# A fused two-layer attention kernel: a new order of work with chunks of 1, 2, 2, 2 and 1 groups, two-operand VectorE forms and split transfers

## The chip, the cores and the metric

The kernel runs on one core of one Trainium2 chip. The metric is the device time of one execution in microseconds (us); a measurement is the median of several executions. Engines are called PE (matrix), DVE (vector), ACT (scalar), POOL (GpSimd) and SP (sync, which issues DMAs); ACT issues DMAs too.

## The reference

The input is `x` of 32 sequences with 32 positions and 128 features. Two layers follow one another.

```python
# layer 0: conditioned transformer block, 16 heads of 8 features
cmod = silu(c) @ w_ada + b_ada                 # shift, scale, gate for both halves
qkv  = modulate(ln(x), shift_msa, scale_msa) @ w_qkv
w    = softmax(q / 8 . k);  y = w @ v
x    = x + gate_msa * (y @ w_proj + b_proj)
h    = gelu(modulate(ln(x), shift_mlp, scale_mlp) @ w_mlp1 + b_mlp1)
x    = x + gate_mlp * (h @ w_mlp2 + b_mlp2)
# layer 1: graph attention, 16 heads, 2 directions, keys are the first 20 positions
self_feat = concat(x, q_exp) @ W_self.T + b_self      # q_exp is 0 where a row of x sums to 0
for d in range(2):
    A    = (adj, or adj with its axes swapped)[:, :, :20, :]
    aff  = where(A.sum(-1) > 0, (q_d . k_d) / sqrt(8), NEG) + (A @ w_bias + b_bias)
    out += einsum(softmax(aff) @ self_feat[:, :20], Wout_d) + bout_d
x = x + relu(self_feat + out)
```

## The kernel before, in words

All arithmetic is float32. The 32 sequences are 8 *groups* of 4 sequences, so a group is 128 tokens. In layer 0 the normalization and the q, k, v products work on *chunks* of groups (`CHUNKS`), here of 1, 1, 2, 2 and 2 groups; from the projection on, everything works on four *mids* of two groups (`MIDS`). One *unit* is the attention of one group (units 0 to 7, layer 0) or of one group and direction (units 8 to 23, layer 1: group 0 has units 8 and 9, and so on). Units are handled in *sets* (`SETS`) that share one softmax pass: sets 0 to 4 belong to layer 0, and sets 5 to 12 to layer 1, one for each group with both directions. Mid m of layer 1 holds the units 8+4m to 11+4m.

A set runs through: `scores` (PE, 32 small products for a group and direction, each two PE instructions since the data is float32) into `ps_s`; in layer 1 `badd` (DVE, adds the bias and frees `ps_s`); `max` (DVE); `sub` (DVE or POOL); per unit `turn` (PE transposes), `exp` (ACT) and `values` (PE); then `recip` and `mult` (DVE). `ya` adds the two directions, `oT` transposes back, `fin1` and `fin2` (DVE) finish, and `store` writes.

The order is written out: `ORDER` is one list of (stage, key), `ON` says which engine does a step, and each engine takes its own steps from the list in that order, waiting on semaphores for what it needs and for buffers to come free. Nothing overtakes on an engine. `BANKS` gives each product one of four PSUM banks.

The names that the change touches:

- `stats` (DVE) takes mean and variance of a chunk, `rstd` (POOL) the power -0.5, `apply` normalizes (here POOL, one instruction per group), `dense xnT` transposes on PE, `take xnT` (DVE) multiplies by the scale and `shift` adds the shift; then come the products q, k and v and their `take`s. `vmask` writes a masked copy of v. A `take` of `k` is four masked copies, here all on ACT.
- `spread (v1, m)` copies the layer-1 values of mid m into the block layout `Vz1` by eight small DMAs, all issued by SP. `Vz1` has two slots (`V1_RING`), so the spread of mid 2 waits until the `values` of mid 0 (units 8 to 11) are done, and that of mid 3 until those of mid 1 (units 12 to 15) are. The `values` of a mid wait for its spread.
- `WARM` transposes of the identity run on PE at the start.
- `nmr` is minus mean times rstd, which ACT needs for a normalization by scale and bias.

## Time and profile before

| | |
|---|---|
| runs shown | 99.52, 98.32, 98.66 us; median 98.66 us |
| profiled execution | 97.58 us, span 95.8 us |
| granted TensorE clock, mean | 0.995 |
| busy in the span | PE 80.1 us, DVE 71.3, POOL 56.1, ACT 39.6 |

The span runs from the first to the last instruction of the profiled execution; 1.8 us of its own time lie around it. Busy times say how loaded an engine is, not what ends the kernel: that is read from waits and from the chain of work that ended last. A matmul's busy time includes its latency, so a PE that is busy without a break may still not be at its peak.

### The profile page before, as it was taken

To read this page: it belongs to the slowest core of one execution; us is meant where nothing else is said; L and a number is where in the kernel's file an instruction comes from. 1 tells how busy PE (TensorE), PEld (TensorE's weight loads), DVE (VectorE), ACT (ScalarE), POOL (GpSimd) and SP (SyncE) were. 2 spreads that over 40 slices of the span, in tenths; PEclk is the share of its full clock that TensorE was granted. 3 is DMA by queue.
4 is the path that set the end of the run, shared out by engine and by line. 5 is a ranking of instruction groups with operands and counts; after the bars stand their busy time and mean duration, and the time that the engine had idled before them with its cause. 6 is when DMAs were issued, how large, how long until landed. Compare 5 with 4: busy or idle time off the path is not lost.

```text
span 95.8 us, 4031 instructions
## 1 busy us (share of the span) xinstructions
PE 80.1 (84%) x1762; PEld 63.7 (66%) x1762; DVE 71.3 (74%) x176; ACT 39.6 (41%) x87; POOL 56.1 (59%) x70
## 2 busy tenths in 40 slices
PE   3519799899769999999999999999998698649620
PEld 3319487576558647787898887998787586537510
DVE  3980858987887999858856578986998779487491
ACT  0910076947506007955244406607383073225200
POOL 6799949999970983953530551964049176733030
PEclk9999999999999999999999999999999999999997
DMA  1999991000000000000000210002100011121303
GB/s 32 253 355 270 388 405 62 7 0 0 10 7 0 7 0 0 7 0 0 3 7 0 43 24 17 3 0 38 31 14 7 7 43 31 31 43 21 114 10 110
DMA packets 4034, 5.75 MB, mean 60 GB/s; under 512 B 720, under 2 KB 3152, under 8 KB 3888
## 3 DMA queue, kind: packets, MB, share of 16 engines
q1 hardware_dynamic: 3584, 4.96, 17.0%
q10 hardware_dynamic: 432, 0.52, 1.5%
q8 instruction: 14, 0.23, 1.1%
q14 instruction: 4, 0.03, 0.1%
HBM read 4.22 MB, written 0.52 MB: 50 GB/s over the span
## 4 chain that ended last, share of the span: by engine, by line
PE 56%; SPq 13%; POOL 10%; DMA 7%; DVE 6%; issue 5%; POOLq 0%
SPq L797 12%; PE ps_b L956 8%; PE ps_b L962 7%; PE ps_s L1018 6%; DMA w_ada_sb<-in_w_ada 5%; POOL Vz L734 4%; PE ps_b L885 4%; PE ps_b L969 4%; PE ps_b L973 4%; PE ps_b L1062 3%; PE ps_b L902 3%; PE ps_b L936 3%; PE ps_b L975 2%; PE ps_b L1054 2%; PE ps_b L980 2%
## 5 line engine op out<-in xcount | busy, mean ns | idle before, releaser
L712 POOL TENSOR_TENSOR E<-E,neg_max 128x640 f32<-128x640 f32 x7 | 9.4, 1346 | 5.6 <-DVE neg_max L1334 5.6
L1148 ACT ACTIVATE PT<-ps_b 120x384 f32<-120x384 f32 x16 | 7.3, 488 | 11.8 <-PE ps_b L1029 11.5
L744 POOL TENSOR_TENSOR Kb<-k_raw,head_mask 128x640 f32<-128x640 f32 x5 | 6.3, 1254 | 8.9 <-DVE k_raw L1246 5.4
L1089 ACT ACTIVATE Kb<-ps_b,head_mask 128x256 f32<-128x256 f32 (+1 forms) x20 | 7.0, 438 | 7.6 <-PE ps_b L936 7.6
L1326 DVE TENSOR_TENSOR E<-ps_s,bias_head 128x640 f32<-128x640 f32 x8 | 6.6, 825 | 3.8 <-PE ps_s L1018 3.0
L1104 ACT ACTIVATE hidden<-ps_b,cols 128x256 f32<-128x256 f32 x16 | 7.3, 474 | 4.9 <-PE ps_b L956 4.7
L936 PE MATMUL ps_b<-xm,w_qkv_sb 128*128 128x256 f32 (+1 forms) x30 | 8.4, 421 | 0.5 <-DVE xm L696 0.5
L956 PE MATMUL ps_b<-xm,w_rest_sb 128*128 128x256 f32 x32 | 8.7, 387 | 0.0
L734 POOL TENSOR_TENSOR Vz<-v_raw,quad_mask 128x1152 f32<-128x1152 f32 (+1 forms) x5 | 8.5, 1729 | 0.0
L1054 PE MATMUL ps_b<-Vz,PT 120*32 120x54 f32 (+1 forms) x384 | 5.7, 207 | 3.3 <-issue 2.3
L1029 PE MATMUL ps_b<-ident,E 128*120 128x128 f32 x48 | 7.0, 279 | 1.2 <-DVE home_a L1370 1.2
L1054 PEld LDWEIGHTS ps_b<-Vz,PT 120*32 120x32 f32 (+1 forms) x384 | 4.8, 109 | 4.4 <-issue 4.1
L962 PE MATMUL ps_b<-hidden,w_rest_sb 128*128 128x256 f32 x32 | 7.7, 382 | 0.0
L1018 PE MATMUL ps_s<-Kb,home_b 32*32 32x80 f32 x512 | 7.4, 239 | 0.0
L936 PEld LDWEIGHTS ps_b<-xm,w_qkv_sb 128*128 128x128 f32 x30 | 5.8, 238 | 2.1 <-DVE xm L1201 0.8
L706 POOL TENSOR_TENSOR xT<-gated,xT 128x256 f32<-128x256 f32 x5 | 3.6, 730 | 6.1 <-DVE gated L1219 6.1
L846 POOL TENSOR_TENSOR rstd<-var_eps,minus_half 128x2 f32<-128x2 f32 (+1 forms) x9 | 6.1, 678 | 1.9 <-DVE var_eps L1180 1.7
L717 POOL TENSOR_TENSOR home_a<-home_a 128x128 f32<-128x128 f32 x6 | 2.7, 457 | 7.2 <-DVE home_a L1370 7.2
L696 POOL TENSOR_TENSOR xm<-xm,cmod 128x256 f32<-128x256 f32 (+1 forms) x7 | 4.1, 585 | 4.8 <-DVE xm L1201 4.8
L1018 PEld LDWEIGHTS ps_s<-Kb,home_b 32*32 32x32 f32 x512 | 5.5, 103 | 1.8 <-issue 1.3
L1334 DVE TENSOR_REDUCE neg_max<-E 128x32 f32<-128x640 f32 x8 | 6.5, 817 | 0.2
L852 POOL TENSOR_SCALAR xn_tok<-x_tok,meanvar,rstd 128x128 f32<-128x128 f32 x8 | 6.4, 801 | 0.5
(102 smaller groups left out, 191.1 us busy)
## 6 DMA issues: line engine op xcount, KB each, us to landing
w_rest_sb<-in_w_rest SPq DMA_DIRECT2D x1, 1088.0 KB, 10.1
home_a<-in_adj SPq DMA_DIRECT2D x2, 448.0 KB, 6.8
Vz<-v_raw SPq DMA_DIRECT2D x16, 33.8 KB
home_a<-in_adj SPq DMA_DIRECT2D x1, 512.0 KB, 8.1
xT<-in_xT SPq DMA_DIRECT2D x1, 512.0 KB, 10.6
out<-gated SPq DMA_DIRECT2D x3, 128.0 KB, 1.8
x_tok<-in_x_tok ACTq DMA_DIRECT2D x1, 256.0 KB, 4.5
w_ada_sb<-in_w_ada SPq DMA_DIRECT2D x1, 256.0 KB, 4.9
```

Of the source, the lines that this page charges most:

```text
L712: return engine.tensor_tensor(e, e, less_max(key), ALU.add)
L734: return engine.tensor_tensor(Vz0[:, :, bs, :, :].rearrange("p i b j w -> p i (b j w)"), v0_raw[:, bs, :, :].rearrange("p b j w -> p (b j ...
L797: sp.dma_start(Vz1[to, k, i, c:c1, 0:nb, :, :].rearrange("p c b d w -> p c (b d w)"), v1_raw[of, j:j + c1 - c, bs, :, :].rearrange("p c b ...
L936: return pe.matmul(ps[:, 0:n], w, xm[:, bs, :], start=True, stop=True)
L956: return pe.matmul(ps[:, 0:n], w_mlp1_sb[:, name[2], :], xm[:, bs, :], start=True, stop=True)
L962: ins = pe.matmul(ps[:, 0:n], w_mlp2_sb[:, j, :], hidden[:, h % HID_RING, j, 0:n], start=(j == js[0]), stop=(j == js[-1]))
L1018: ins = pe.matmul(ps_s[QUAD * b:QUAD * b + QUAD, j, u * nk:(u + 1) * nk], qT, Kb, start=True, stop=True)
L1029: ins = pe.transpose(ps[0:KR, c * P:(c + 1) * P], E1[:, r, u, c * KR:(c + 1) * KR], ident[:, :])
L1054: ins = pe.matmul(ps[QUAD * b:QUAD * b + QUAD, o + c * SIX * CW:o + c * SIX * CW + w], PT[0:rows, r, c, b * S:(b + 1) * S], V, start=True, ...
L1089: return act.activation(Kb0[:, part, bs, :], ps_bs, ACT.Copy, scale=head_mask[:, 1, part:part + 1])
L1104: return act.activation(hidden[:, h % HID_RING, j, 0:n], ps[:, 0:n], ACT.Gelu_apprx_tanh, bias=cols[:, R_MLP1 + j:R_MLP1 + j + 1])
L1148: ins = act.activation(PT[0:KR, r, 0:CH, :], ps[0:KR, 0:CH * P].rearrange("p (j t) -> p j t", t=P), ACT.Exp)
```

## The change

The code gains four things. `apply` can run on ACT (with `nmr` computed on DVE for layer 0 too). Three kinds of small DVE operation of one input (`plus1`, `masks`, `var_eps`) become `scalar_tensor_tensor` with two inputs that give the same values. A spread is cut in halves of four DMAs, each half a step of its own, and two of the eight halves are issued by ACT. `warm` steps can stand anywhere in PE's order, each two transposes of the identity.

```diff
+SPREAD_PARTS = [[(0, 0, 0, 0, CH), (1, 1, 0, 0, CH), (4, 0, CH, 0, 1), (4, 1, CH, 1, 1)],
+                [(2, 2, 0, 0, CH), (3, 3, 0, 0, CH), (5, 2, CH, 0, 1), (5, 3, CH, 1, 1)]]
-CHUNKS = [(0, 1), (1, 2), (2, 4), (4, 6), (6, 8)]
-SETS = [(0,), (1,), (2, 3), (4, 5), (6, 7), (8, 9), (10, 11), ...
-XLOADS = [(0, 1), (1, 4), (4, 8)]
-LOADS_SP = ['cols', 'ada0', 'qkv', 'ada1', 'adj0', 'adj1', 'adj2', 'rest', 'xT']
+CHUNKS = [(0, 1), (1, 3), (3, 5), (5, 7), (7, 8)]
+SETS = [(0,), (1, 2), (3, 4), (5, 6), (7,), (8, 9), (10, 11), ...
+XLOADS = [(0, 1), (1, 3), (3, 8)]
+LOADS_SP = ['cols', 'ada0', 'qkv', 'adj0', 'adj1', 'adj2', 'ada1', 'rest', 'xT']
-WARM = 6
+WARM = 11
- 'apply': 'pool',
+ 'apply': 'act',
- 'resid2': 'pool',
+ 'resid2': 'dve',
- 'shift': 'pool',
+ 'shift': 'dve',
+ 'sub': 'dve',
+ ('sub', 7): 'pool',
...
+ ('spread', ('v1', 2, 0)): 'act',
+ ('spread', ('v1', 3, 0)): 'act',
+        def spread_half(engine, name, m, half):
...
+            for i, quad, j, c, n in SPREAD_PARTS[half]:
+                engine.dma_start(Vz1[M * i:M * i + M, k, i, c:c + n, 0:nb, :, :].rearrange("p c b d w -> p c (b d w)"),
+                                 v1_raw[QUAD * quad:QUAD * quad + M, j:j + n, bs, :, :].rearrange("p c b d w -> p c (b d w)"))\
+                      .then_inc(spread_done["v1", m, half], 16)
+                elif stage == "warm":
+                    for i in range(2):
+                        ins = pe.transpose(ps_s[:, i, 0:P], ident[:, :], ident[:, :])
+                elif stage == "apply":
+                    for s in fresh("act", ("nmr", (0, key)), ("rstd", (0, key))):
+                        act.wait_ge(*s)
+                    for g in range(*CHUNKS[key]):
+                        ins = act.activation(xn_tok[:, g, :], x_tok[:, g, :], ACT.Identity, bias=nmr[:, 0, g:g + 1],
+                                             scale=rstd[:, 0, g:g + 1])
-                return dve.tensor_scalar(var_eps[:, layer, g0:g1], meanvar[:, layer, g0:g1, 1], LN_EPS, None, ALU.add)
+                v = meanvar[:, layer, g0:g1, 1]
+                return dve.scalar_tensor_tensor(out=var_eps[:, layer, g0:g1], in0=v, scalar=LN_EPS, in1=v, op0=ALU.add,
+                                                op1=ALU.max)
```

The whole `ORDER` and `BANKS` are new. Layer 1 now takes its sets in the order 6, 8, 5, 7, 10, 9, 11, 12 (before 5 to 12). On DVE there now also stand the `sub` of sets 5 and 6 (before that of set 7 alone), all four `resid2` (before one), most of the `shift`s of layer 0 (chunks 0, 1, 2 and 4; before 1 and 2) and one `vmask`, and two of the three layer-1 key masks (`k1mask`) that were on DVE are on POOL; three of the four layer-1 normalizations (`take x1tok`) move from DVE to ACT. Three places show how the rows of an engine moved.

PE at the start, before: identity transposes (`ident`), the modulation product (`w_ada_sb`), transposes of the normalized input (`xn_tok`), the q, k, v products (`w_qkv_sb`) and the first scores.

```order
L986 MATMUL ps_s<-ident 128x128 x6
L912 MATMUL ps_b<-silu_c,w_ada_sb 128x32 x6
L885 MATMUL ps_b<-ident,xn_tok 128x128 x4
L936 MATMUL ps_b<-xm,w_qkv_sb 128x256 x2
L885 MATMUL ps_b<-ident,xn_tok 128x128 x2
L936 MATMUL ps_b<-xm,w_qkv_sb 128x128 x3
L1018 MATMUL ps_s<-Kb,selfT 32x128 x32
```

The same place after the change.

```order
L992 MATMUL ps_s<-ident 128x128 x11
L918 MATMUL ps_b<-silu_c,w_ada_sb 128x32 x2
L998 MATMUL ps_s<-ident 128x128 x4
L891 MATMUL ps_b<-ident,xn_tok 128x128 x5
L942 MATMUL ps_b<-xm,w_qkv_sb 128x256
L891 MATMUL ps_b<-ident,xn_tok 128x128 x2
L998 MATMUL ps_s<-ident 128x128 x2
L942 MATMUL ps_b<-xm,w_qkv_sb 128x256 x3
L1027 MATMUL ps_s<-Kb,selfT 32x128 x32
```

The second part of the modulation product (4 of its 6) no longer stands ahead of the transposes, more identity transposes do, and the products ahead of the first scores are four of 256 columns instead of two of 256 and three of 128.

DVE in the first microseconds, before: statistics (`stats`, `meanvar`, `var_eps`), the modulation (`cmod`) and the first modulated input (`xm`).

```order
L1191 TENSOR_TENSOR cmod<-ps_b,cols 128x64
L1175 BN_STATS stats<-x_tok 128x6 x2
L1178 BN_AGGR meanvar<-stats 128x2 x2
L1180 TENSOR_SCALAR var_eps<-meanvar 128x2
L1201 TENSOR_TENSOR xm<-ps_b,cmod 128x256
L696 TENSOR_TENSOR xm<-xm,cmod 128x256
```

The same place after the change.

```order
L1197 BN_STATS stats<-x_tok 128x6 x2
L1200 BN_AGGR meanvar<-stats 128x2 x2
L1203 SCALAR_TENSOR_TENSOR var_eps<-meanvar 128x2
L1310 SCALAR_TENSOR_TENSOR nmr<-meanvar,rstd 128x2
L1310 SCALAR_TENSOR_TENSOR nmr<-meanvar,rstd 128x1
L1215 TENSOR_TENSOR cmod<-ps_b,cols 128x64
L1225 TENSOR_TENSOR xm<-ps_b,cmod 128x256
L704 TENSOR_TENSOR xm<-xm,cmod 128x256
```

The `nmr` that ACT's normalization waits for stands behind the statistics of four chunks; a third `nmr` row, alike, is left out here.

ACT in the last third, before: exponentials (`PT`), and copies of the layer-1 keys (`k_raw`) and queries (`home_b`).

```order
L1148 ACTIVATE PT<-ps_b 120x384 x2
L1115 ACTIVATE k_raw<-ps_b,bk_scaled 128x160
L1148 ACTIVATE PT<-ps_b 120x384
L1110 ACTIVATE home_b<-ps_b,cols 128x256
L1115 ACTIVATE k_raw<-ps_b,bk_scaled 128x160
L1110 ACTIVATE home_b<-ps_b,cols 128x256
L1148 ACTIVATE PT<-ps_b 120x384 x12
```

The same place after the change.

```order
L1170 ACTIVATE PT<-ps_b 120x384 x6
L1124 ACTIVATE k_raw<-ps_b,bk_scaled 128x160 x2
L1119 ACTIVATE home_b<-ps_b,cols 128x256
L776 DMA Vz<-v_raw 20x3x144 x2
L776 DMA Vz<-v_raw 20x144 x2
L1170 ACTIVATE PT<-ps_b 120x384 x3
L776 DMA Vz<-v_raw 20x3x144 x2
L776 DMA Vz<-v_raw 20x144 x2
L1170 ACTIVATE PT<-ps_b 120x384 x7
```

Four DMA issues (half a spread of mid 2) now stand ahead of the last ten exponentials, and four more (mid 3) ahead of the last seven.

## Rows read from the trace of the kernel before

**Rows 1.** Page, part 1: busy us, share of the span, instructions.

```profile
PE 80.1 (84%) x1762; PEld 63.7 (66%) x1762; DVE 71.3 (74%) x176; ACT 39.6 (41%) x87; POOL 56.1 (59%) x70
```

**Rows 2.** Busy time by stretches: PE, PEld, DVE, ACT, POOL, clock, DMA share, GB/s.

```profile
30.00:40.00 10.00, 9.89 (x208) 6.63 (x207) 8.95 (x28) 4.72 (x9) 6.84 (x7) 1.00 0.02 3
60.00:70.00 10.00, 10.00 (x200) 8.57 (x179) 8.44 (x15) 4.98 (x10) 4.94 (x4) 1.00 0.10 19
80.00:90.00 10.00, 6.74 (x255) 5.37 (x247) 6.43 (x14) 3.71 (x8) 3.88 (x6) 1.00 0.18 47
```

**Rows 3.** Chain that ended last, in order of time: start us, us, what.

```profile
64.64 0.43 PE ps_b L973 x2
65.07 0.27 PE ps_b L975 x2
65.34 0.33 PE ps_b L1029 x3
65.67 0.84 PE ps_s L1018 x49
...
71.10 0.54 PE ps_b L980 x4
...
74.98 0.32 PE ps_b L1054 x9
...
75.32 0.81 SPq L797
...
81.76 0.81 SPq L797
...
87.39 1.84 DMA Vz<-v_raw
```

**Rows 4.** Waits of SP's queue: what waited for whom, us, times, longest.

```profile
SPq L797 <- PE ps_b L1054: 4.8, 1, 4.8
```

**Rows 5.** Timeline of the last values: start us, us, engine, line.

```profile
89.36 1.25 PE L1054 MATMUL ps_b<-Vz,PT 120*32 120x54 f32 x96 [0.82 <-DMA Vz<-v_raw]
```

**Rows 6.** Timeline of the first 20 us: start us, us, engine, line.

```profile
0.80 1.38 ACTq L1070 DMA_DIRECT2D x_tok<-in_x_tok  x3
...
6.25 0.49 DVE L1175 BATCH_NORM_STATS2 stats<-x_tok 128x6 f32<-128x128 f32 x2 [0.21 <-DMA x_tok<-in_x_tok]
...
10.85 2.04 PE L936 MATMUL ps_b<-xm,w_qkv_sb 128*128 128x256 f32 x4 [0.55 <-DVE xm L696]
...
14.42 1.04 POOL L870 CAST home_b<-home_a 112x1024 f32<-112x1024 int32 x1
14.49 0.99 DVE L1180 TENSOR_SCALAR var_eps<-meanvar 128x2 f32<-128x2 f32 x1
...
19.11 1.13 PE L936 MATMUL ps_b<-xm,w_qkv_sb 128*128 128x256 f32 x4
```

**Rows 7.** Groups of instructions by line and shape: count, busy us, mean ns, idle before.

```profile
L1148 ACT ACTIVATE PT<-ps_b 120x384 f32<-120x384 f32 x16 | 7.3, 488 | 11.8 <-PE ps_b L1029 11.5
L1326 DVE TENSOR_TENSOR E<-ps_s,bias_head 128x640 f32<-128x640 f32 x8 | 6.6, 825 | 3.8 <-PE ps_s L1018 3.0 <-PE ps_b L1029 0.5
L1334 DVE TENSOR_REDUCE neg_max<-E 128x32 f32<-128x640 f32 x8 | 6.5, 817 | 0.2
L852 POOL TENSOR_SCALAR xn_tok<-x_tok,meanvar,rstd 128x128 f32<-128x128 f32 x8 | 6.4, 801 | 0.5
L734 POOL TENSOR_TENSOR Vz<-v_raw,quad_mask 128x1152 f32<-128x1152 f32 x3 | 6.3, 2114 | 0.0
...
L1359 DVE RECIPROCAL rden<-ps_b 128x32 f32<-128x32 f32 x11 | 3.9, 352 | 2.7 <-PE ps_b L1054 2.6
...
L1235 DVE STREAM_TRANSPOSE v_raw<-ps_b 128x512 f32<-128x512 f32 x4 | 2.8, 706 | 1.4 <-PE ps_b L980 1.4
```

**Rows 8.** Line 712 on POOL: shortest, median, longest ns, first and last start.

```profile
L712 POOL TENSOR_TENSOR E<-E,neg_max x7: 1272/1273/1785, 59.4 to 85.3; 128x640 f32<-128x640 f32 x7
```

**Rows 9.** Timeline at 59.4 us.

```profile
59.44 1.78 POOL L712 TENSOR_TENSOR E<-E,neg_max 128x640 f32<-128x640 f32 x1 [2.76 <-DVE neg_max L1334]
```

More of the change, by code:

```diff
@@ L68 @@
 K_POOL = set()
-WARM = 6
+WARM = 11
 ON = {'adjf': 'pool',
- 'apply': 'pool',
+ 'apply': 'act',
  'badd': 'dve',
  'bdir': 'dve',
- 'bhead': 'act',
+ 'bhead': 'pool',
+ 'bks': 'act',
  'bturn': 'dve',
@@ L86 @@
  'mult': 'dve',
+ 'nmr': 'dve',
  'pen': 'dve',
@@ L99 @@
  'store': 'sp',
- 'sub': 'pool',
+ 'sub': 'dve',
  'turn': 'pe',
@@ L103 @@
  'vmask': 'pool',
+ 'warm': 'pe',
  'ya': 'pool',
  'zero': 'pool',
+ ('adjf', 2): 'act',
+ ('bhead', 1): 'act',
  ('k1mask', (0, 1)): 'dve',
- ('k1mask', (1, 0)): 'dve',
- ('k1mask', (1, 1)): 'dve',
  ('resid1', 2): 'dve',
  ('resid1', 3): 'dve',
- ('resid2', 3): 'dve',
- ('shift', (0, 1)): 'dve',
- ('shift', (0, 2)): 'dve',
- ('sub', 0): 'dve',
- ('sub', 1): 'dve',
- ('sub', 2): 'dve',
- ('sub', 3): 'dve',
- ('sub', 4): 'dve',
- ('sub', 7): 'dve',
+ ('shift', (0, 3)): 'pool',
+ ('shift', (1, 1)): 'pool',
+ ('shift', (1, 2)): 'pool',
+ ('spread', ('v1', 2, 0)): 'act',
+ ('spread', ('v1', 3, 0)): 'act',
+ ('sub', 7): 'pool',
+ ('sub', 8): 'pool',
+ ('sub', 9): 'pool',
+ ('sub', 10): 'pool',
+ ('sub', 11): 'pool',
+ ('sub', 12): 'pool',
  ('take', (('cmod', 0), 0)): 'dve',
@@ L174 @@
  ('take', (('q', 0), 0)): 'act',
[L175 to L176 removed]
+ ('take', (('q', 1), 0)): 'dve',
+ ('take', (('q', 2), 0)): 'act',
  ('take', (('q', 3), 0)): 'act',
@@ L185 @@
  ('take', (('q1', 3, 0), 0)): 'act',
- ('take', (('q1', 3, 1), 0)): 'act',
+ ('take', (('q1', 3, 1), 0)): 'dve',
  ('take', (('rowsum', 0), 0)): 'dve',
@@ L783, in _ @@
                 if stage == "spread":
[L784 to L799 removed]
+                    spread_half(sp, "sp", *key[1:])
                 else:
@@ L1046, in _ @@
                         m = mid_of(g)
-                        for s in fresh("pe", ("spread", ("v1", m))):
+                        for s in fresh("pe", ("spread", ("v1", m, 0)), ("spread", ("v1", m, 1))):
                             pe.wait_ge(*s)
@@ L1092, in take_part @@
                 if kind == "x1tok":
-                    for s in fresh("act", ("nmr", h), ("rstd", (1, h))):
+                    for s in fresh("act", ("nmr", (1, h)), ("rstd", (1, h))):
                         act.wait_ge(*s)
@@ L1096, in take_part @@
                         ins = act.activation(xn_tok[:, g, :], ps[:, (g - g0) * P:(g - g0 + 1) * P], ACT.Identity,
-                                             bias=nmr[:, g:g + 1], scale=rstd[:, 1, g:g + 1])
+                                             bias=nmr[:, 1, g:g + 1], scale=rstd[:, 1, g:g + 1])
                     return ins
@@ L1112, in take_part @@
                 d = name[2]
-                for s in fresh("act", ("gbias", 0)):
+                for s in fresh("act", ("bks", 0)):
                     act.wait_ge(*s)
@@ L1127, in _ @@
                     continue
+                elif stage == "spread":
+                    spread_half(act, "act", *key[1:])
+                    continue
+                elif stage == "bks":
+                    for s in fresh("act", ("load", "cols")):
+                        act.wait_ge(*s)
+                    ins = act.activation(bk_scaled[:, :], cols[:, R_K:R_K + DIRS], ACT.Copy, scale=C ** -0.5)
+                elif stage == "apply":
+                    for s in fresh("act", ("nmr", (0, key)), ("rstd", (0, key))):
+                        act.wait_ge(*s)
+                    for g in range(*CHUNKS[key]):
+                        ins = act.activation(xn_tok[:, g, :], x_tok[:, g, :], ACT.Identity, bias=nmr[:, 0, g:g + 1],
+                                             scale=rstd[:, 0, g:g + 1])
                 elif stage == "adjf":
@@ L1243, in take_part @@
                 if kind == "k1":
-                    for s in fresh("dve", ("gbias", 0)):
+                    for s in fresh("dve", ("bks", 0)):
                         dve.wait_ge(*s)
@@ L1280, in _ @@
                 elif stage == "nmr":
-                    g0, g1 = MIDS[key]
-                    for s in fresh("dve", ("rstd", (1, key))):
+                    layer, p = key
+                    g0, g1 = norm_chunk(layer, p)
+                    for s in fresh("dve", ("rstd", key)):
                         dve.wait_ge(*s)
-                    ins = dve.scalar_tensor_tensor(out=nmr[:, g0:g1], in0=meanvar[:, 1, g0:g1, 0], scalar=-1.0,
-                                                   in1=rstd[:, 1, g0:g1], op0=ALU.mult, op1=ALU.mult)
+                    ins = dve.scalar_tensor_tensor(out=nmr[:, layer, g0:g1], in0=meanvar[:, layer, g0:g1, 0], scalar=-1.0,
+                                                   in1=rstd[:, layer, g0:g1], op0=ALU.mult, op1=ALU.mult)
                 elif stage == "apply":
```

415 lines of the change are left out of this document (204 added, 211 removed), and 10 rows, old and new, of the table ORDER.

## Prediction, before the changed kernel ran

> **What bounds the kernel now.** I read the busy time by stretches first. PE is busy without a gap from 30 to 70 us, and falls to 6.74 of 10 us at 80 [rows 2]; over the span it is the busiest engine [rows 1]. So there are three stages: a head in which PE waits, a middle that PE's work sets, and a tail. The chain of work that ended last confirms it. In the middle it is one PE piece behind another; at 75.30 us (I call it T0: the last `values` of units 8 to 11 end) it leaves PE, and SP issues sixteen DMAs one after another, eight from 75.32 and eight from 81.76; the last one lands 1.84 us after its issue, at 89.22 [rows 3]. SP had waited 4.8 us for those `values` [rows 4], since the two slots of `Vz1` were taken. The last four units' `values` run from 89.36 to 90.61 [rows 5], and 5.15 us later the span ends. From T0 to the end are 20.5 us, 13.9 of them issue and landing.
>
> **The tail.** The issues are as many as before, about 0.77 us each by the two runs of eight (81.76 - 75.32 = 6.44 with the wait between; 87.39 - 81.76 = 5.63). But half of each spread goes to ACT's queue. Walking the new order from T0:
> - PE takes two `q1` and a `k1` (0.43 + 0.27 + 0.43 [rows 3]), and ACT copies the last at about T0 + 1.65. ACT then issues four DMAs (3.1 us, to 4.75) while SP issues the other four. Behind ACT's stand the exponentials of units 13, 12 and 19 (0.49 each [rows 7], to 6.2), and with them the `values` 13 and 12 (to 6.05).
> - Now mid 1 is free. ACT issues four more (6.25 to 9.35), landed at 11.2 with the 1.84 of rows 3, and only then the exponentials of 18, 16, 17, 20 and 21 (to 11.8).
> - DVE is the second queue. From T0 to the `max` of set 12 it has 16 operations: three `badd` and four `max` (0.82 each, 5.7 together [rows 7]) and nine from 0.35 to 0.72 ([rows 7] give the two ends; 3.9 together), so the `max` ends at 9.85 with what is unfinished at T0. `sub` 12 on POOL takes 1.27 [rows 8], to 11.1; two `turn`s (0.33 each) end at 12.0 with the hand-over, and exponential 23 at 12.7.
> - The last `values` (0.31 a unit: 1.25 for four [rows 5]) end at 13.4, and 5.15 follow: 18.6, or 18.9 with 0.3 for hand-overs that I rounded off.
>
> So T0 to the end takes 18.9 instead of 20.5: **-1.6 us**. Both spreads have landed 1 us before they are wanted, and what comes last instead is DVE's queue, with ACT's 0.2 us behind it. Removing 6 us of serial issue gives back far less than 6, because the softmax chains of the last three sets are as long.
>
> **Work moved behind T0.** In the new order two `q1`, one `k1` and one `v1` stand behind T0 (0.86 + 0.27 + 0.54 = 1.67 us [rows 3]), and two units' `turn`s have gone ahead of it (0.66). In a stage that PE's work sets, T0 itself comes 1.0 us earlier: **-1.0 us**. The walk above has the moved work in it.
>
> **The head.** The first `k` product starts at 10.85 [rows 6]. In the new order it needs chunk 1 alone, but `nmr` of chunk 1 stands behind the statistics of four chunks, and two of these wait for the third load of `x`, which lands at about 6.25 or a little later (it grows from 4 to 5 groups) [rows 6]. Two statistics of 0.97 us each, from there, end at 8.3; ACT's normalization, transpose, scale and shift lead to a first product at about 10.5. That is 0.3 us earlier, not more, though POOL loses 6.4 us of `apply` (0.80 each [rows 7]). Next, `var_eps` took 0.99 us at 14.49, until the cast on POOL ended at 15.46 [rows 6]; the two-input form should take its usual 0.17, and POOL's `rstd` behind it comes 0.8 us earlier. The second modulation part no longer stands ahead of the transposes. Against that `adj` now loads ahead of it, and POOL has still 8.5 us of `vmask` and casts in the same 20 us.
>
> The PE clock decides the rest. Two-instruction products of 256 columns took 0.51 us each at 10.85 and 0.28 at 19.11 (2.04 and 1.13 for four [rows 6]), while the page lists the clock as full. By these times PE worked at its lower level, 1.2 GHz, in the first, and at 2.4 GHz in the second; it had been busy almost without a break from 10.85. If the new warm-up raises it by 10 us, my walk of the first attention has 1.5 us more PE work done at 36 us than before; if it rises where it did, none. I take **-0.5 us**, between 0 and -1.5, nearer to the unchanged case.
> The Trainium skill says in TensorE: Matmul & The Clock Gate, Part 4 (PE-mode transpose), that transposes do not count as PE activity for the clock. All the added warm-up is transposes. By that rule the head's gain is 0 and the time 0.5 us above my forecast; the row at 10.85, slow behind six such transposes, does not speak against it.
>
> **DVE in the middle.** DVE gets three `resid2`, more `shift`s, one more `sub`, `nmr` and a `vmask`, and loses three normalizations and two key masks: about +2 us on 71.3 [rows 1]. From the first layer-1 scores to T0 I count 12.9 us of DVE work for 14.0 us of PE work, 92%, where the stretch from 60 to 70 has 8.44 of 10 [rows 2]. PE will wait for it now and then: **+0.7 us**, between 0 and 1.5. The eleven identity transposes and two of the warm steps stand in time in which PE waits for `x`, and cost nothing; the third warm step stands among products and costs 0.2 us, which is in the head's term. The other edits (`bhead` to POOL, `bks`, `consts`) lie under PE's middle.
>
> **Sum.** -1.6 - 1.0 - 0.5 + 0.7 = -2.4 us. Against its own time that is 95.8 to 93.4 of span, 97.6 to 95.2 of the profiled execution; against the median of 98.66, which lies 1.1 above that execution, **96.3 us**, -2.4%. A measurement of this kernel tells about 2% (2 us) from no change.
>
> **Rivals.**
> - *POOL blocks DVE.* The moved `shift`, `sub`, `resid2` and `vmask` read two operands from SBUF on DVE, beside POOL's long ones. In the trace the one `sub` on POOL that ran beside such a DVE operation took 1.78 us instead of 1.27 [rows 8, 9], so 0.5 us for one meeting. A `shift` behind a fresh `vmask` (2.11 [rows 7]) would lose up to 2.1, ahead of `max` and `sub` of set 2, and three or four meetings on the path cost 1.5 to 2.5 us: 98.3 at the middle. The DVE queue would then be the bound from 20 us on. For it: DVE is already the tighter queue. Against it: most DVE work there reads PSUM.
>  SBUF — State Buffer, section Who interferes with whom, of the Trainium skill states this as a rule: a DVE instruction with two SBUF inputs and a GpSimd one that reads SBUF exclude each other for a whole instruction. It speaks for this rival, and by it the two-operand `var_eps` would still wait for a cast (0.8 us more than my sum), though not for a memset.
> - *ACT's issues hold the exponentials (slower).* In the tail ACT has 0.2 us of slack. If an issue there takes as long as SP's, the sum holds; ACT's own early ones took 0.46 [rows 6]. If both queues hinder one another and each issue doubles to 1.5 us, the two groups of four delay units 13 to 22 by 3.1 us each: 6.2 - 0.2 = +6.0, so 102.3 us, slower. The point from which it decides the sign is 0.77 + 2.4/8 = 1.1 us an issue.
> - *Faster still.* The clock rises early (-1.0 more), DVE's load hides (-0.7) and the `var_eps` wait was on the path of all later chunks (-0.8): 93.8 us.
> - *The change does not do what it says.* ACT's half of a spread stands behind copies and exponentials, so it may be issued later than SP's would have been. In my walk it is 1.65 us late for mid 2 and on time for mid 3; it would have to be 1 us later before a landing is last.
>
> **How the numbers follow.** Forecast case (95.0 to 97.4) 0.47; POOL blocks DVE (97.4 to 99.5) 0.24; faster still (below 95.0) 0.17; slow issues on ACT (above 99.5) 0.12. Faster than 96.7 (2%) is the third and three quarters of the first: 0.52. Slower than 100.6 is most of the last: 0.10. The rest, 0.38, is within 2%. Eight in ten: 93.9 to 99.8.
>
> **What the new profile would show.** The chain of the tail without SP; the last spread landed about 1 us ahead of the last `values`; T0 to the end about 19 us. T0 at 73.8 or a little before. First `k` product at 10.5; its instructions at 0.5 or 0.28 us tell the clock. `var_eps` never above 0.3 us. PE busy nearly all of 37 to 73, DVE near 9 of 10 in the last third. I am wrong if ACT's issues exceed 1 us, if PE shows gaps for DVE of more than 2 us together in the middle, or if the first attention ends later than before.

## The result, and the profile after

The changed kernel took 101.12 us (median of 4 runs, 100.09 to 101.57) beside 98.49 us for the kernel before on the same chip: ratio 1.031, interval 1.025 to 1.037. It is slower; I had forecast 96.3 us and given this side a tenth. The same kernel timed again in a later group of runs gave a ratio of 1.018 (1.006 to 1.029). Single executions of either kernel scatter by 1.5% and more; ratios are of undisturbed runs, medians of all runs, so the two do not always match. The profiled execution took 101.2 us, its span 99.4.

The windows that answer to [rows 2], and the same for the second profile of the same kernel and for before, from the end of T0's `values` to the end of the last ones (busy time of PE, PE's loads, DVE, ACT and POOL, then granted clock and DMA):

```profile
30.00:40.00 10.00, 8.96 (x220) 6.31 (x218) 7.87 (x26) 4.39 (x9) 5.15 (x7) 1.00 0.02 4
40.00:50.00 10.00, 9.26 (x46) 7.13 (x46) 7.78 (x27) 5.16 (x13) 2.29 (x5) 1.00 0.00 0
80.00:90.00 10.00, 7.16 (x261) 5.59 (x260) 6.01 (x12) 2.90 (x7) 5.49 (x7) 1.00 0.18 44
...
76.00:94.40 18.40, 15.55 (x530) 12.63 (x525) 11.74 (x25) 5.24 (x12) 9.04 (x11) 0.91 0.15 38
```

The second profile of the changed kernel:

```profile
76.20:92.45 16.25, 14.26 (x525) 11.46 (x526) 11.89 (x25) 5.12 (x12) 9.04 (x11) 1.00 0.14 36
```

The kernel before:

```profile
75.25:90.60 15.35, 11.97 (x523) 9.98 (x522) 10.84 (x25) 5.45 (x12) 6.80 (x8) 1.00 0.17 45
```

In the middle PE is no longer without gaps (8.96 and 9.26 where before had 9.89 and 9.96). And behind T0 it has 14.3 us of work up to the end of the last `values` (the second profile; the first, at a lower clock, has 15.6), 2.3 more than before. T0 is at 76.08 us (before 75.30; the sum of my terms puts it at 74.5) and T0 to the end takes 23.3 us (before 20.5; my walk 18.9). These two errors, 1.6 and 4.4, are the whole 6.0 us between my span of 93.4 and 99.4.

PE in the tail, timeline of the profile after (start, duration, instruction, and in brackets the idle time ahead and what ended it; "issue" means that PE waited for nothing that the profile shows):

```profile
75.66 0.40 PE L1063 MATMUL ps_b<-Vz,PT 120*32 120x54 f32 x17 [0.83 <-issue]
...
81.96 0.79 PE L1063 MATMUL ps_b<-Vz,PT 120*32 120x54 f32 x41 [0.26 <-ACT PT L1170]
83.49 0.27 PE L1063 MATMUL ps_b<-Vz,PT 80*32 80x36 f32 x7 [0.74 <-issue]
...
88.64 0.55 PE L1038 MATMUL ps_b<-ident,E 128*120 128x128 f32 x3 [1.75 <-ACT PT L1170]
...
91.20 1.54 PE L1038 MATMUL ps_b<-ident,E 128*120 128x128 f32 x6
92.67 1.75 PE L1063 MATMUL ps_b<-Vz,PT 120*32 120x54 f32 x96
```

ACT's own queue in the same stretch:

```profile
77.51 3.86 ACTq L776 DMA_DIRECT2D Vz<-v_raw  x4
81.41 1.26 ACT L1170 ACTIVATE PT<-ps_b 120x384 f32<-120x384 f32 x3 [3.51 <-PE ps_b L1063]
83.87 4.18 ACTq L776 DMA_DIRECT2D Vz<-v_raw  x4
88.10 1.64 ACT L1170 ACTIVATE PT<-ps_b 120x384 f32<-120x384 f32 x4 [5.43 <-issue]
```

Where [rows 3] had sixteen DMAs of SP in the chain, there is now this: the `values` of unit 12 end at 83.76 (T0 + 7.7), ACT issues its second four for 4.18 us, exponential 18 stands behind them, and the `turn` of unit 20 waits 1.75 us for it, since it takes the bank of `turn` 18 and 19. After that wait the granted clock fell to the half from 90.4 to 93.8 us: 48 products took 1.07 us, where the second profile, at full clock, has 0.73, six `turn`s 1.54 instead of 0.87, and 96 products 1.75 instead of 1.43. Together 1.3 us; the second profile, without this fall, has T0 to the end in 21.2.

The middle and the head:

```profile
11.00 1.19 PE L942 MATMUL ps_b<-xm,w_qkv_sb 128*128 128x256 f32 x2
12.84 2.68 PE L942 MATMUL ps_b<-xm,w_qkv_sb 128*128 128x256 f32 x6
15.46 1.07 PE L1027 MATMUL ps_s<-Kb,selfT 32*32 32x128 f32 x64
...
37.48 0.41 PE L891 MATMUL ps_b<-ident,xn_tok 128*128 128x128 f32 x2 [1.04 <-ACT xn_tok L1105]
```

The first `k` product starts at 11.00 ([rows 6]: 10.85; I said 10.5) and its instructions are still slow ones. The first scores start at 15.46, 0.9 later than before's 14.56. At 36.4 PE waits 1.04 us for a normalization on ACT, and that for `nmr` on DVE, which the new order puts behind the copy of a projection and a bias. Three more waits of this kind (0.23, 0.22, 0.29) follow up to 49.5; before had none there.

### The profile page after: what moved, and what is told of

Same layout as the page of the kernel before. It is cut to its first block, busy times and chain, and to the rows that moved or that the text cites. A ratio compares the mean times of both kernels' runs of the same rounds, so it can differ in the third digit from the quotient of the medians.

```text
span 99.4 us, 4074 instructions
## 1 busy us (share of the span) xinstructions
PE 84.0 (85%) x1773; PEld 66.2 (67%) x1773; DVE 72.1 (73%) x180; ACT 45.0 (45%) x102; POOL 48.0 (48%) x59
## 4 chain that ended last, share of the span: by engine, by line
PE 63%; DVE 11%; ACTq 8%; ACT 5%; issue 5%; DMA 5%; POOL 0%
PE ps_s L1027 8%; ACTq L776 8%; PE ps_b L942 6%; PE ps_b L962 6%; PE ps_b L968 5%; PE ps_b L1063 5%; PE ps_b L891 5%; DMA x_tok<-in_x_tok 5%; PE ps_b L1038 5%; PE ps_b L975 4%; PE ps_b L1041 3%; PE ps_b L908 3%; PE ps_b L979 3%; PE ps_b L981 2%; PE ps_b L1071 2%
## 5 line engine op out<-in xcount | busy, mean ns | idle before, releaser
L752 POOL TENSOR_TENSOR Kb<-k_raw,head_mask 128x640 f32<-128x640 f32 x7 | 9.8, 1409 | 13.9 <-ACT k_raw L1124 12.9
L891 PE MATMUL ps_b<-ident,xn_tok 128*128 128x128 f32 x16 | 4.1, 350 | 5.9 <-ACT xn_tok L1148 3.7
L720 POOL TENSOR_TENSOR E<-E,neg_max 128x640 f32<-128x640 f32 x6 | 7.7, 1289 | 2.5 <-DVE neg_max L1360 2.5
L1385 DVE RECIPROCAL rden<-ps_b 128x32 f32<-128x32 f32 (+1 forms) x13 | 4.4, 336 | 6.1 <-PE ps_b L1063 6.1
L1063 PE MATMUL ps_b<-Vz,PT 120*32 120x54 f32 (+1 forms) x384 | 7.2, 225 | 1.8 <-issue 1.6
L1063 PEld LDWEIGHTS ps_b<-Vz,PT 120*32 120x32 f32 (+1 forms) x384 | 6.0, 122 | 3.6 <-issue 2.5
L725 POOL TENSOR_TENSOR home_a<-home_a 128x128 f32<-128x128 f32 x8 | 3.7, 468 | 7.9 <-DVE home_a L1396 7.9
L1038 PEld LDWEIGHTS ps_b<-ident,E 128*120 128x120 f32 x48 | 5.7, 147 | 2.6 <-ACT PT L1170 1.9
L891 PEld LDWEIGHTS ps_b<-ident,xn_tok 128*128 128x128 f32 x16 | 2.0, 167 | 7.9 <-ACT xn_tok L1148 4.4
L1243 DVE SCALAR_TENSOR_TENSOR gated<-ps_b,cols,cmod 128x256 f32<-128x256 f32 x8 | 3.8, 481 | 4.5 <-PE ps_b L968 3.9
```

The source lines that it names most:

```text
L720: return engine.tensor_tensor(e, e, less_max(key), ALU.add)
L752: return engine.tensor_tensor(Kb1[:, m % K1_RING, d, :, 0:(g1 - g0) * UB, :].rearrange("p i b k -> p i (b k)"), k1_raw[:, d, bs, :].rearra ...
L891: ins = pe.transpose(ps[:, i * P:(i + 1) * P], src(i), ident[:, :])
L1038: ins = pe.transpose(ps[0:KR, c * P:(c + 1) * P], E1[:, r, u, c * KR:(c + 1) * KR], ident[:, :])
L1063: ins = pe.matmul(ps[QUAD * b:QUAD * b + QUAD, o + c * SIX * CW:o + c * SIX * CW + w], PT[0:rows, r, c, b * S:(b + 1) * S], V, start=True, ...
```

## Experiments

**All spreads on SP.** The first edit has a flaw: the order of the steps holds the first half of mid 3 ahead of the second half of mid 2, harmless on two queues, but not on one.

```diff
- ('spread', ('v1', 2, 0)): 'act',
- ('spread', ('v1', 3, 0)): 'act',
```

> The kernel after, with one thing undone: the two half spreads that ACT issued (mid 2 and mid 3) are issued by SP again, so SP issues all sixteen DMAs of the tail one after another. If ACT's issues hold the exponentials (my theory now: two groups of about 4 us on ACT, and exponential 18 waits 5.4 us), T0 stays at 76.1 us, exponential 18 comes some 4 us earlier, and T0 to the end falls from 23.3 to about 20.5 us: about 98.3 us, 2.8 less than the kernel after. Rival: PE's work and its lower clock, or DVE's queue, set the tail, or SP's sixteen serial issues cost as much as ACT's do; then 101 us, no change.

106.57 us, ratio 1.071 (1.053 to 1.088). SP waits for the `values` of mid 1 until 83.8, and only then issues the rest of mid 2; PE stands idle for 5.8 us:

```profile
92.00 0.71 PE L1061 MATMUL ps_b<-Vz,PT 120*32 120x54 f32 x24 [5.83 <-DMA Vz<-v_raw]
```

It says nothing on ACT's issues, but what one step in the wrong place of a queue costs. The mended order, and one with only mid 2's first half on ACT:

```diff
- ('dense', ('oT', 0)), ('spread', ('v1', 3, 0)), ('recip', 7),
+ ('dense', ('oT', 0)), ('recip', 7),
...
- ('exp', 16), ('spread', ('v1', 3, 1)), ('max', 12),
+ ('exp', 16), ('spread', ('v1', 3, 0)), ('spread', ('v1', 3, 1)), ('max', 12),
```

> The kernel after with all sixteen DMAs of the tail on SP, now in the order mid 2 first half, second half, mid 3 first half, second half (in e1_spread_sp the first half of mid 3 stood ahead of the second of mid 2, waited for the values of mid 1 and held it). Mended theory: the release of mid 1 comes at about T0 + 7.5 us because PE has that much work ahead of it in the new order (4.0 us in the kernel before), eight issues of 0.77 and a landing of 1.84 make T0 + 15.6, the last values and 5.15 us follow: T0 to the end about 22 us, 98.5 to 99.5 us in all, 1 to 2 below the kernel after, whose exponential 18 waits for ACT's issues. Rival: the halves on ACT do help; then T0 to the end is over 24 us and the time over 101.5.

> The kernel after with the first half of mid 3 back on SP (behind the second half of mid 2); ACT keeps the first half of mid 2. Theory: exponential 18 starts at T0 + 8.5 us instead of T0 + 12.0, the clock does not fall in the tail, the last landing is at T0 + 15.7 as in e6_sp_in_order, and the time is that of e6 within 0.5 us. Rival (ACT's issue of mid 2 alone costs): 1 us or more above e6.

e6: 101.41 us, ratio 1.019 (1.005 to 1.033). e7: 100.83 us, 1.017 (0.999 to 1.035). In e6 exponential 18 starts at 84.4, 3.7 us earlier than in the profile after, the `values` of unit 12 still end at 83.7, and the last landing is now late:

```profile
92.39 1.74 PE L1061 MATMUL ps_b<-Vz,PT 120*32 120x54 f32 x96 [2.85 <-DMA Vz<-v_raw]
```

T0 to the end is 23.0 in e6 (0.5 of it by a lower clock in the row above: 1.74 us, where e7 has 1.25), 21.9 in e7, 23.3 and 21.2 in the two profiles of the kernel after: the theory that ACT's issues alone make the loss falls. They hold the exponentials as the rival said, but the landing that they bring forward is worth as much. What all these versions have is the release of mid 1 at T0 + 7.3 to 7.7. Up to it PE is busy but for 0.7 to 1.0 us: in e6 one gap of 0.89 that ends in "issue", so its work alone would end at T0 + 6.4.

**The code without the order**, and the halves on ACT in the old order, late and early.

> The kernel before with the new code and the old order, banks, chunks and engines: two-operand forms of var_eps, plus1 and masks, spreads in halves that SP issues both, bk_scaled on ACT. My theory: var_eps falls from 0.99 us at its worst to 0.16, and the time is that of the kernel before or up to 0.5 us less (98.0 to 98.5). Rival: the forms or the new tile layout cost part of the loss; then over 99.5 us.

98.51 us, ratio 1.004 (0.998 to 1.011): no change that can be told. The forms gain nothing, and `var_eps` is not freed. In e3, DVE and POOL:

```profile
14.74 0.98 DVE L1198 SCALAR_TENSOR_TENSOR var_eps<-meanvar 128x2 f32<-128x2 f32 x1
```

```profile
14.67 1.04 POOL L871 CAST home_b<-home_a 112x1024 f32<-112x1024 int32 x1
```

The two-operand form takes 0.98 us beside the cast, like the one-operand form (0.99 in [rows 6]), and ends with it. I had put it at 0.17. The rule of the Trainium skill that I set against this term (SBUF — State Buffer, Who interferes with whom) agrees with this row. In the kernel after all nine `var_eps` take 0.16 us, but by their place: none stands beside a cast. A `shift` stands there instead, and takes 1.11 us, where the other of its shape takes 0.27:

```profile
15.17 1.11 DVE L704 TENSOR_TENSOR xm<-xm,cmod 128x128 f32<-128x128 f32 x1
```

```diff
+ ('spread', ('v1', 2, 0)): 'act',
+ ('spread', ('v1', 3, 0)): 'act',
```

> e3_forms, and ACT issues the first half of the spreads of mid 2 and mid 3, at the places of the old order, behind exponentials 15 and 21. Theory (ACT's issues hold the exponentials only where some stand behind them): only a few stand behind, an issue on both queues at once takes about 1.0 us instead of 0.77, the last spread lands 1.5 to 2 us earlier than by SP alone, and the time is 1 to 2 us below e3_forms. Rival (halves on ACT are bad wherever they stand): 1 us or more above e3_forms. Second rival (two queues only share one issuer): no change.

101.77 us (99.93 to 103.80). Behind exponential 21, ACT issues the half of mid 3 at 91.0 (in an execution of 103.8 us), where SP in the kernel before had issued all of it by 88.1:

```profile
91.00 3.28 ACTq L773 DMA_DIRECT2D Vz<-v_raw  x4
```

I had expected a gain of 1 to 2 us here, which failed. With mid 3's half alone, behind exponential 15:

```diff
+ ('spread', ('v1', 3, 0)): 'act',
- ('exp', 21), ('spread', ('v1', 3, 0)), ('spread', ('v1', 3, 1)),
+ ('values', 15), ('spread', ('v1', 3, 0)), ('sub', 10), ...
+ ('exp', 21), ('spread', ('v1', 3, 1)),
```

> e3_forms with only the first half of mid 3 on ACT, and early: behind exponential 15 instead of behind exponential 21 (e4 had it there and ACT issued it at 91.0 us, 9 us after SP would have). Theory: ACT issues it from 79.4 to 83.3 us, the last spread lands near 87 instead of 89.3, exponentials 16 to 19 come up to 2.5 us later without being last, and the exponentials of 20 to 23 (to 89.1) become the bound: time within 0.5 us of e3_forms. Rival (an ACT issue holds what counts): 1 us or more above e3_forms. Second rival (the landing alone is the bound): 1.5 us or more below.

97.94 us, ratio 0.998 (0.990 to 1.006): the landing is no longer waited for, and there is no change that can be told, as expected. What stands ahead of the last `values` now are PE's own work, a gap of 1.07 us ended by "issue" and one of 1.14 for DVE, not the exponentials that I had named. Between e4 and e11 lie 3.8 us in the medians and 2.7 in the shortest executions. The place of a half on ACT's queue is the main difference, but e4 has mid 2's half there too, and two "issue" gaps of 1.66 and 1.86 us, e11 of 1.92 and 1.07. A well placed half gains nothing that can be told.

**`nmr` early**, in the kernel after.

```diff
- ('pen', 0), ('take', (('proj', 0), 0)), ('bdir', 0), ('turn', 7), ('nmr', (1, 1)),
+ ('pen', 0), ('nmr', (1, 1)), ('take', (('proj', 0), 0)), ('bdir', 0), ('turn', 7),
```

> The kernel after with nmr of the second pair of groups in layer 1 right behind pen on DVE, ahead of one bias add and one copy. Theory (DVE's order costs in the middle): PE's gap of 1.04 us at 36.4 shrinks, T0 comes 0.5 to 1.0 us earlier, and the time is 0.5 to 1.0 us below the kernel after. Rival: the gap is given back before T0 by PE's next wait; then no change.

99.33 us, ratio 1.011 (0.996 to 1.025), which is not told apart from the kernel after's second ratio (below, 1.018). In the trace the gap of 1.04 us at 36.4 is gone and T0 is at 74.77 instead of 76.08 (76.18 in the second profile); 0.2 to 0.4 of that lead was there ahead of the gap, so some 1.1 us are `nmr`'s. With the first half of mid 2 on SP again (ACT keeps that of mid 3):

> e5_nmr (the kernel after with nmr early) with the first half of mid 2 back on SP; ACT keeps the first half of mid 3. Theory: exponentials 13 and 12 no longer wait 3.5 us behind ACT's four issues, but PE has other work until then, so mid 1 is free at T0 + 7.0 instead of 7.4; SP needs until T0 + 6.4 for mid 2 and then joins ACT: 0.3 to 0.8 us below e5_nmr. Rival (two queues at once always win): up to 1 us above e5_nmr.

99.30 us, ratio 1.005 (0.995 to 1.015), not told apart from e5. Unit 12's `values` end at T0 + 7.3, not 7.0, though nothing on ACT is waited for: 6.4 us of PE's work and a gap of 0.92 lie ahead of them. T0 is at 75.59 here, 0.8 later than in e5: 0.5 was there by the scores at 27.0, and the gap ahead of T0 is 1.10 us, not 0.80.

**The kernel after, once more.**

> The kernel after itself, once more, on the chip of this group, to see which of its marks repeat. If the loss is what my reading says (bias product nmr late in the middle, late release of mid 1, exponential 18 behind ACT's issues), T0 is again near 76 us and T0 to the end 22.5 to 23.5, about 101 us. What may change from run to run: the clock in the last 8 us and the gaps of 0.2 to 1.4 us inside runs of values. If the tail is then 21.5 or less, part of the 23.3 was that run's alone.

99.96 us, ratio 1.018 (1.006 to 1.029). T0 76.18, T0 to the end 21.2: of the 23.3, 2.1 were that execution's. Four issues on ACT took 3.73 instead of 4.18, the gap in unit 12's `values` was 0.44 instead of 0.74, and the clock stayed full.

**Identity transposes in PE's idle time** at 5.5 to 9.2 us: 34 and 18 full ones.

```diff
+ ('warm', 2), ('warm', 3), ..., ('warm', 19), ('dense', ('xnT', 1)),
```

> The kernel after with 34 more identity transposes on PE behind its last early warm step; they add nothing to the output and fill PE's idle time from 5.5 to 9.2 us, ahead of the first transposes of x. Theory: the granted clock, which rose at 5.1 us and fell to the half at 8.5 us in that idle time, stays full until 15 us, the q, k, v products take 0.28 instead of 0.51 us, and the first scores come 1 us or more earlier: about 100 us. Rival: the head is set by DVE and ACT, not by PE's clock; then the first scores stay at 15.5 us and the time at 101.

> e2_fill with 18 more identity transposes instead of 34 (nothing is added to the output). In e2 the fill ended at 12.2 us, 3 us after the normalized input was there, so the first product came 2.6 us later than after's, and still the time fell by 2 us. Theory: this fill ends at 9 to 10 us and PE's clock is full from about 10.5 us; first product at 11 us or before, first scores at 14.5 us (15.5 after), T0 at 75 us, 1 us less than e2: about 98.4 us. Rival: the gain of e2 is not the head's but the tail's (the clock there did not fall); then the time is that of e2 or more, whatever the first scores do.

e2: 99.36 us, 1.011 (0.999 to 1.023). e8: 99.03 us, 1.008 (1.002 to 1.013). Both lie clear of the kernel after's first ratio (1.031), but their intervals overlap that of the second (1.018), though the first scores come at 16.6 and 16.4, a microsecond later than after's. In e2 the products take 0.28 us each from 13.63 on, so full clock; in e8 it fell again and the product gain was lost, yet the time is the same. Thus what they may gain is not in the head. In the old order the fill gave nothing that can be told:

```diff
-WARM = 6
+WARM = 13
+ ('dense', ('cmod', 0)), ('warm', 0), ('warm', 1), ('warm', 2),
```

> e3_forms (the order of before) with identity transposes where PE idles in the head: 13 at the start instead of 6, and 6 behind the first modulation product; they add nothing to the output. Theory: PE then works from 1.6 to 9 us nearly without a break, its clock is full before the first k product at 11 us, four products of 256 columns take 1.13 instead of 2.05 us, first scores at 13.3 instead of 14.6, and the time falls by 0.5 to 1.3 us below e3_forms: about 97.5 us. Rival (transposes do not raise the clock, or the head is set by DVE and POOL): the products stay at 0.51 us each, or the scores come earlier and T0 does not; no change.

99.39 us beside 99.42 for before; the products at 10.58 still take 2.04 us for four, the clock is low there in spite of the fill.

**The gaps inside runs of `values`.** The kernel before has such gaps too; these are two of its three, the first with the last 9 products of T0's `values` behind it:

```profile
74.98 0.28 PE L1054 MATMUL ps_b<-Vz,PT 120*32 120x54 f32 x9 [1.12 <-issue]
...
85.99 0.62 PE L1054 MATMUL ps_b<-Vz,PT 120*32 120x54 f32 x38 [1.21 <-issue]
```

What e2 and e8 changed is where the gaps marked "issue" stand. The kernel after, e8 (18 more instructions ahead) and e2 (34 more), in that order:

```profile
83.49 0.27 PE L1063 MATMUL ps_b<-Vz,PT 80*32 80x36 f32 x7 [0.74 <-issue]
```

```profile
77.33 0.62 PE L1063 MATMUL ps_b<-Vz,PT 120*32 120x54 f32 x35 [1.40 <-issue]
...
84.62 0.47 PE L1063 MATMUL ps_b<-Vz,PT 80*32 80x36 f32 x25 [0.30 <-issue]
```

```profile
83.37 0.63 PE L1063 MATMUL ps_b<-Vz,PT 120*32 120x54 f32 x41 [0.22 <-issue]
```

Behind unit 12's gap stand 7, 25 = 7 + 18 and 41 = 7 + 34 products; behind the one before T0 stand 17 and 35 = 17 + 18, and with 34 more it is gone. To tell the number of instructions from the time that they take, 34 small transposes (32x32) go into the same idle time:

```diff
+                    if key == 2:
+                        for i in range(34):
+                            ins = pe.transpose(ps_s[0:QUAD, i % HJ, 0:QUAD], ident[0:QUAD, 0:QUAD], ident[0:QUAD, 0:QUAD])
```

> The kernel after with 34 small identity transposes (32x32, some 0.03 us each) on PE in its idle time from 5.5 to 9.2 us, where e2 had 34 full ones; nothing is added to the output. PE shows gaps of 0.4 to 1.4 us inside runs of values that nothing in the trace explains; in e2 (34 more transposes) and e8 (18 more) they stood exactly 34 and 18 instructions earlier in the same run. Theory A (PE waits for its code, which comes in blocks of a fixed number of instructions): here they move as in e2, the one before T0 vanishes, and the time falls by 0.5 to 1.5 us without any change of the clock in the head. Theory B (e2 gained by the clock alone): products stay at 0.6 us, the time at 100 to 101.

98.56 us (12 runs), ratio 0.999 (0.993 to 1.004): some 2 to 3% of the kernel after, from 34 instructions that compute nothing. Its gaps:

```profile
28.28 0.27 PE L891 MATMUL ps_b<-ident,y_tok 128*128 128x128 f32 x1 [0.93 <-issue]
37.46 0.41 PE L891 MATMUL ps_b<-ident,xn_tok 128*128 128x128 f32 x2 [1.04 <-ACT xn_tok L1108]
...
81.88 0.63 PE L1066 MATMUL ps_b<-Vz,PT 120*32 120x54 f32 x41 [0.37 <-issue]
```

The clock rose earlier here, and the first scores came at 14.49, 1.0 before after's. But a gap of 0.93 at 28.3 takes that back: at 37.46 the kernel stands where after stood (37.48). T0 is then at 75.32, 0.8 earlier. The gap of 0.83 ahead of it has shrunk to some 0.3 and moved into the scores (64 in 1.24 us instead of 0.91). In e17 (below), with the same 34 instructions, it is a row of its own, with 3 scores and 48 `values` behind it up to T0, 51 = 17 + 34:

```profile
74.62 0.32 PE L1030 MATMUL ps_s<-Kb,home_b 32*32 32x80 f32 x3 [0.31 <-issue]
```

T0 to the end is 20.7; the wait for exponential 18 is 0.84 instead of 1.75 and 1.18. But the gaps add up to 1.6 us (0.93, 0.3 and 0.37), as in after: what changed is where they stand, not their sum. And the mean granted clock is 0.991 or more in eleven of the twelve executions, 0.938 to 0.998 in the kernel after's ten. So a share of the gain may be the clock's, and no run separates the two.

Before's order with 42 and 64 small transposes at the start:

```diff
+            for i in range(42):
+                pe.transpose(ps_s[0:QUAD, i % HJ, 0:QUAD], ident[0:QUAD, 0:QUAD], ident[0:QUAD, 0:QUAD])
```

> e11_act_early (before's order, ACT issues one half of mid 3 early) with 42 small identity transposes on PE at the start, in idle time. Theory A: the gap 9 instructions ahead of T0 (1.1 to 1.9 us in before, e3 and e11) moves 42 instructions up, into the last ones of the scores or just ahead of them, and shrinks below 0.5; T0 comes 0.5 to 1 us earlier, the time falls to about 97.3 us. Rival: the gap stays where it is in the work, or appears as large in another place; then the time is e11's (97.9).

> As e13 with 64 small transposes, to tell a block boundary from chance: by theory A the gap before T0 stands 64 instructions earlier, in the scores of set 10, and its size may be anything from 0 to 1.5; the time lies between e13's and e11's. Rival: no relation of place and number.

e13: 99.34 us, ratio 0.990 (0.982 to 0.999), not told apart from e11. The gap ahead of T0 is gone there, but others stand at 30.1 (1.78 us) and 83.8 (1.87), so the rival was right. e14: 100.73 us, ratio 1.010 (1.003 to 1.016). The place obeys, the size doesn't: e11 has a gap of 1.07 with 38 products of units 16 to 19 behind it; e13 has one with 80 = 38 + 42, and e14 one with 102 = 38 + 64 (3 of the scores, 3 `turn`s and 96 `values`):

```profile
87.98 1.06 PE L1061 MATMUL ps_b<-Vz,PT 80*32 80x36 f32 x80 [0.77 <-issue]
```

```profile
77.91 0.34 PE L1025 MATMUL ps_s<-Kb,home_b 32*32 32x80 f32 x9 [2.05 <-issue]
...
82.83 0.84 PE L1025 MATMUL ps_s<-Kb,home_b 32*32 32x80 f32 x57 [1.43 <-issue]
...
86.67 0.33 PE L1025 MATMUL ps_s<-Kb,home_b 32*32 32x80 f32 x3 [0.98 <-issue]
```

Counting records, e14's gaps stand 126 and 127 matmuls apart, before's last two 381 = 3 x 127, after's 253 = 2 x 126.5. But e14's gaps sum to 6.0 us (before's to 3.3, after's to 1.6), and I had expected it between e11 and e13: which places are good can't be read from the place alone.

**The code queue by itself.** 512 small products at PE's start.

```diff
+            for i in range(512):
+                pe.matmul(ps_s[0:QUAD, i % HJ, 0:QUAD], ident[0:QUAD, 0:QUAD], ident[0:QUAD, 0:QUAD], start=True, stop=True)
```

> The kernel after with 512 small products of the identity (32x32, f32) at PE's start, which go nowhere; they are a thousand matmul records of the size of the scores, with no wait among them. It measures the suspected cause by itself. 
Neither theory's number came (one execution, 150.53 us): the products gave 1024 records, which ran in 54.82 us without a gap, 53.5 ns each, four times slower than the scores. At 6.8 us for 128 they can't show a wait for code. But the DMA part of the page can. Kernel after, and e18:

```profile
q8 instruction: 14, 0.23, 1.0%
```

```profile
q8 instruction: 22, 0.36, 1.0%
```

Eight packets more, 0.13 MB, for 1024 records: one of 16 KB for each 128 matmuls. And they can be placed in time. This is the answer for 73.0 to 73.5 us in the kernel after, 2 us ahead of the gap before T0:

```profile
q8 instruction: 1, 0.02, 13.0%
```

The next ones are in the half microseconds from 76.5, 81.0 and 84.5, in the kernel before in those from 72.5, 76.0, 79.5, 83.0 and 87.0: 3.5 to 4.5 us apart where PE runs through scores and `values`. Each gap of these two kernels in that stretch ends 2 to 3 us behind such a packet, and the next packet follows it by 1 to 1.5 us. That PE waits for its code in these gaps is my reading of three things: the places move one for one with the records, the distances are multiples of 126 to 127, and a packet comes for each 128. No trace shows the wait itself, and most of the 14 packets go with no gap.

**The two repairs together**, with mid 2's half on SP (e15) and on ACT (e17).

> e12_nmr_act30 (the kernel after with nmr early and the first half of mid 2 on SP) with the 34 small transposes of e16. It had a gap of 1.10 us before T0 and one of 0.92 in the values of unit 12. By theory A both go or shrink: 0.7 to 1.5 us below e12, about 98.2 us. If the gains do not add up, the time stays at e12's 99.3.

> e15 with the first half of mid 2 on ACT again, that is the kernel after with two edits only: nmr early, and the 34 small identity transposes in PE's idle time. Theory: the two edits are worth 1.2 us (e5) and 1.5 to 2.5 us (e16) and add up, and the half of mid 2 is worth nothing either way: within 0.5 us of e15, 97.7 to 98.5, faster than the kernel before by about 1%. Rival (the half of mid 2 on ACT holds exponentials 13 and 12): 1 us above e15.

e15: 98.18 us, ratio 0.987 (0.979 to 0.996). e17: 98.03 us (12 runs), ratio 0.992 (0.986 to 0.998). Together they are 3 to 4% below the kernel after and about 1% below the kernel before. e15 has T0 at 74.23 and T0 to the end in 21.6, and "issue" gaps of 1.7 us in all, which is again no less than the kernel after's.

## Why the prediction was wrong

**Tail, -1.6 us: wrong in size and sign.** It is the term that failed. The walk followed ACT's and DVE's queues from T0 and took PE as there when wanted. But PE itself has 14.3 us of work between T0 and the last `values` in the new order, against 12.0 before; with the 5 us behind them that alone is 19.3, more than my 18.9. On it come waits of 1.9 us in the second profile: 1.18 for exponential 18 behind ACT's issues, 0.44 of "issue" and 0.26 for ACT, 21.2 in all. The first profile's 2.1 more are some 1.3 of low clock and 0.8 of longer waits, and belong to that execution. So the work that I left out turns my gain of 1.6 into one of 1.2 at most (20.5 to 19.3), and the waits on top make it a loss of 0.7. The prices were there in [rows 3], and a sum over PE's order would have shown the first part. The points of the walk: unit 12's `values` end T0 + 6.05, measured 7.7 and 7.4 (e12, without ACT's first issues, 7.3, so PE's work and its gap set it); second issues 3.1 us, measured 4.2 and 3.7; exponential 18 at T0 + 9.35, measured 12.0 and 11.3; then 4.05 us to the end of the last `values`, measured 6.3 and 5.0. DVE, which I named as last, ended none of PE's waits between T0 and the last `values`.

**Work moved behind T0, -1.0 us.** The move is real, but its size was under-counted and it isn't a gain: PE's work behind T0 grew by 2.3 us, not 1.0. The products are as counted (1.7 us less 0.8 for six `turn`s). The rest lies, as far as I can place it, in pieces that I priced at their best: single units' `values` (24 records in 0.46 us, where 96 take 1.25) and one set of scores of 1.3 to 1.4 us instead of 0.9. At T0 itself the term fits: 75.3 - 1.0 for the work, + 0.9 head, + 1.8 waits in the middle, - 1.2 for smaller "issue" gaps (0.83 against 0.92 and 1.12) is 75.8, an estimate, and 76.08 was measured. The sum put T0 at 74.5; the 73.8 in my list of signs left out the +0.7 of the middle.

**Head, -0.5 us: measured +0.9** at the first scores. The clock was granted in full from 5.1 to 8.5 us, behind 11 to 15 identity transposes and four small products, but PE then stood idle until 9.25, and the products from 11.00 to 15.3 ran at the half level, 1.2 GHz (six records in 2.68 us; in e2, at full clock, in 1.68). The statement of the Trainium skill that I set beside this term (TensorE: Matmul & The Clock Gate, Part 4: transposes do not count as PE activity) forecast no gain, and none came; but the reason differs, since the clock did rise behind transposes. e2 shows it best:

```profile
4.80 1.06 PE L918 MATMUL ps_b<-silu_c,w_ada_sb 128*128 128x32 f32 x4 [0.60 <-DMA w_ada_sb<-in_w_ada]
5.68 6.66 PE L998 MATMUL ps_s<-ident 128*128 128x128 f32 x38
```

From 5.9 us on PE had nothing but these transposes; 7 of them ran in the microsecond from 9 us, and 12 in that from 11 us. The second profile of the kernel after has the same transposes as the first and its clock did not rise at 5.1 (four took 1.09 us, not 0.78), yet the first scores come at 15.49. And the two-operand form of `var_eps` gained nothing (e3); what kept it at 0.16 us in the kernel after is its place.

**DVE in the middle, +0.7 us.** PE does wait there as said, but for 1.8 us, and not because DVE is full (7.87 of 10 us from 30 to 40, before 8.95): one wait of 1.04 is a single step in the wrong place, by e5's trace worth about 1.1 us of T0.

**Rivals.** "ACT's issues hold the exponentials" is what the tail shows: 0.93 to 1.05 us an issue, near the 1.1 from which I let it decide, and ACT without an exponential for 5.4 and 4.7 us ahead of number 18. But e6, without any of them, and e7, without the second four, are not told apart from the kernel after: SP's late landing costs as much. "POOL blocks DVE" showed in e3's `var_eps` and in the `shift` of 1.11 us; its share of the time wasn't isolated. "The change does not do what it says" was wrong for mid 2, whose half ACT issued from T0 + 1.4, and came true for mid 3, from T0 + 7.8 instead of 6.25, though no landing was waited for.

**Not in the sum at all: the "issue" gaps, by my reading PE's waits for its code.** They were in the trace of before: `[1.12 <-issue]` and `[1.21 <-issue]` stand inside runs of `values`, and I read over them. They belong to both kernels (3.3 us in before, 1.6 in after), so they do not by themselves explain the loss. But they move with every edit that adds a PE instruction, and single ones are as large as the effect under study. In the kernel after one of 0.83 stood ahead of T0 and one of 0.44 to 0.74 ahead of the release of mid 1. What stays open: why e13's and e14's gaps grew while after's shrank, and so what share of the 1.031 is the order and what share is such luck; with 34 idle PE instructions 2 to 3% of it go (e16), by the place of the gaps or by the clock, and the late `nmr` step is worth about 1 us of T0 in the trace (e5), though its time alone was not told apart. The second measurement of the same kernel, 1.018, fits its trace: T0 0.9 later than before's and T0 to the end 0.7 longer.
